# A fused convolution, four-bit FFN and expert layer on one core: an earlier start on TensorE, a reordered hand-over to the first down products, and a shorter routing step

## What is computed

```python
# layer 0
h = conv1d(x, weight, 9 taps, 4 groups) + (cond @ c_weight.T)[:, :, None] + bias
w_up, w_down = NF4[codes] * absmax                     # hidden size 2752
y = relu(h @ w_up + b_up + h @ A_up @ B_up)
x = x + y @ w_down + b_down + y @ A_dn @ B_dn
# layer 1
att = softmax(MLP(cond))                               # 8 kernels mixed per batch
z = einsum('boi,bih->boh', sum_k att_k W_k, x) + att @ bias_k
sel = argmax(z @ gate_w.T + gate_b)                    # one expert of 8 for each row
x = x + z @ expert_w[sel].T + expert_b[sel]
```

## Time and profile before

| | |
|---|---|
| timed runs | 1392.38, 1395.85, 1396.06 us (median 1395.85) |
| profiled execution, its own time | 1392.98 us |
| its span, first to last instruction | 1391.4 us |
| PE busy | 1369.3 us (98%) |
| DVE busy | 1114.1 us (80%) |
| ACT busy | 774.9 us (56%) |
| mean granted TensorE clock | 0.997 |

### The profile page before, as it was taken

How to read it: one execution, slowest core, us unless ns; L and a number is a source line. 1 busy time by engine, 2 the same in 40 slices (tenths; PEclk the granted TensorE clock), 3 DMA queues, 4 the chain that set the end, 5 groups by cost and what they waited for, 6 DMA issues and landing times.

```text
span 1391.4 us, 20662 instructions
## 1 busy us (share of the span) xinstructions
PE 1369.3 (98%) x6810; PEld 1126.3 (81%) x6810; DVE 1114.1 (80%) x1127; ACT 774.9 (56%) x872; POOL 227.5 (16%) x251
## 2 busy tenths in 40 slices
PE   8999999999999999999999999999999899999998
PEld 7888888888888888888888888888766588888887
DVE  6869887878887788787877887878643699999996
ACT  5655545454554546445464554555216577777774
POOL 0110000000000000000000000000013257565462
PEclk9999999999999999999999999999999999999999
DMA  6854657487875788666886759876578865969962
GB/s 220 344 227 166 230 208 276 163 293 251 283 255 205 246 267 273 245 254 214 290 245 245 259 196 298 256 279 225 195 295 294 280 180 149 361 194 331 348 173 45
DMA packets 105108, 339.50 MB, mean 244 GB/s; under 512 B 15716, under 2 KB 23404, under 8 KB 105036
## 3 DMA queue, kind: packets, MB, share of 16 engines
q1 hardware_dynamic: 79122, 257.93, 49.9%
q0 software_dynamic: 25376, 80.24, 21.3%
q10 hardware_dynamic: 546, 0.50, 0.1%
HBM read 303.49 MB, written 46.14 MB: 251 GB/s over the span
## 4 chain that ended last, share of the span: by engine, by line
PE 93%; DVE 4%; issue 1%; ACT 1%; DMA 0%; ACTq 0%; POOL 0%; DVEq 0%; POOLq 0%
PE pair L1268 27%; PE pair L1269 27%; PE pair L1270 27%; PE pair L1327 3%; DVE wf L869 1%; PE pair L1603 1%; PE pair L1505 1%; PE pair L1495 1%; PE pair L1437 1%; PE pair L1340 1%; PE pair L1357 1%; PE pair L1517 1%; PE pair L1583 1%; PE pair L1320 0%; PE pair L1394 0%
## 5 line engine op out<-in xcount | busy, mean ns | idle before, releaser
L869 DVE TENSOR_TENSOR wf<-wf,term 128x1024 f32<-128x1024 f32 x308 | 376.6, 1223 | 64.3 <-ACT term L616 49.9
L616 ACT ACTIVATE term<-codes 128x1024 f32<-128x1024 int32 x308 | 320.5, 1055 | 137.2 <-DVE wf L869 137.2
L1268 PE MATMUL pair<-wh,hh 128*128 128x512 f32 x672 | 263.4, 392 | 2.1 <-DVE ring L944 1.4
L1269 PE MATMUL pair<-wl,hh 128*128 128x512 f32 x672 | 262.0, 390 | 0.0
L1270 PE MATMUL pair<-wh,hl 128*128 128x512 f32 x672 | 261.9, 390 | 0.0
L1268 PE MATMUL pair<-ring,wh 128*128 128x512 f32 x624 | 242.9, 389 | 0.0
L1269 PE MATMUL pair<-ring,wh 128*128 128x512 f32 x624 | 242.9, 389 | 0.0
L1270 PE MATMUL pair<-ring,wl 128*128 128x512 f32 x624 | 242.7, 389 | 0.0
L939 DVE TENSOR_TENSOR acc<-acc,pair 128x1024 f32<-128x1024 f32 x160 | 194.6, 1216 | 46.2 <-PE pair L1270 40.3
L803 ACT ACTIVATE whr<-wraw 128x1024 fp32r x176 | 181.7, 1057 | 63.7 <-PE pair L1270 52.1
L1242 DVE TENSOR_TENSOR wlr<-wraw,whr 128x1024 fp32r<-128x1024 f32 x176 | 203.6, 1218 | 0.9 <-issue 0.5
(11 more groups left out here) (202 smaller groups left out, 1558.9 us busy)
## 6 DMA issues: line engine op xcount, KB each, us to landing
ring<-x_parts SPq DMA_DIRECT2D x320, 512.0 KB, 6.7
wraw<-exp_w SPq DMA_DIRECT2D x64, 512.0 KB, 10.0
x_parts<-stage POOLq DMA_DIRECT2D x24, 512.0 KB, 6.7
xg<-exp_b POOLq DMA_DIRECT2D x23, 512.0 KB, 8.1
codes<-codes_up SPq DMA_DIRECT2D x22, 512.0 KB, 7.2
codes<-codes_dn SPq DMA_DIRECT2D x22, 512.0 KB, 6.8
am<-am_dn SPq DMA_DIRECT2D x22, 512.0 KB, 3.8
acc<-x_nat POOLq DMA_DIRECT2D x16, 512.0 KB, 5.3
```

Source lines behind the costliest of these rows:

```text
L616: return nc.scalar.activation(out, codes[:, n % 2], ACT.Relu, scale=scale, bias=-scale * bend)
L869: nc.vector.tensor_tensor(whole(n), whole(n), term[:, e % 2], op).then_inc(term_added, 1)
L1268: mm(ps, ah, bh, start=first, stop=False)
L1269: mm(ps, ah, bl, start=False, stop=False)
```

## The change

- The first thing on PE is nine filler matmuls. Then `conv(0)` starts with its first group, and the context product follows behind that group.
- `low(0, 1)` on DVE comes one convolution batch sooner, and ramp 1 of tile 2 one later.
- Splits of batches 24 and 25 are moved ahead of and between `high`/`low(0, 3)` and `relu`/`hidden_low(0, 1)`.
- `down(0, 0)` waits for the split of batches up to 29 before j = 0 and for all before j = 1, where it waited for all at once. In the first turn `add_down(0, 0, 0)` stands ahead of the ramps, and `add_down(0, 0, 1)` behind two.
- The gates of tiles 13, 14 and 15 write banks 0, 1 and 4; those of 13 and 14 no longer wait for bank 6.
- `ranked` is split into `places` and `digits`, `count_seen` and the marks are moved, and eight tiles instead of seven are marked after `choose(2)`. The filler matmuls between are three instead of six; the last twenty stay.
- SP holds blocks 4 to 7 of expert 1 until the second gather of rows has landed.

```diff
--- before.py
+++ after.py
@@ -303,7 +303,7 @@
         def gate_bank(t):
-            return bank[4 if t == TILES - 1 else 6]
+            return bank[{TILES - 3: 0, TILES - 2: 1, TILES - 1: 4}.get(t, 6)]
...
@@ -438,6 +438,8 @@
                         sp.wait_ge(z_ready, 2 * TILES if e else 4 * kt + 2)
+                        if e and kt == KT // 2:
+                            sp.wait_ge(zg_in[1], 16)
                     sp.dma_start(wraw[:, e % 2, kt], exp_w[e, :, kt]).then_inc(wraw_in[e % 2][kt], 16)
...
@@ -712,9 +714,11 @@
             ramps(0, 3, range(1, 8))
+            conv_high(LATE)
             high(0, 3)
+            conv_high(LATE + 1)
             relu(0, 1)
-            for k in range(LATE, B):
+            for k in range(LATE + 2, B):
                 conv_high(k)
...
@@ -971,9 +975,9 @@
                 elif k == 18:
+                    low(0, 1)
+                elif k == 19:
                     add_ramps(0, 2, (1,))
-                elif k == 19:
-                    low(0, 1)
                 else:
...
@@ -992,20 +996,21 @@
             add_lora(0, 3)
+            conv_low(LATE)
             low(0, 3)
+            conv_low(LATE + 1)
             hidden_low(0, 1)
-            for k in range(LATE, B):
+            for k in range(LATE + 2, B):
                 conv_low(k)
...
                     if isinstance(i, int) and i == k == 0:
+                        add_down(i, k, 0)
                         add_ramps(i, k + 4, (1,))
...
                         add_ramps(i, k + 4, (2,))
-                        add_down(i, k, 0)
-                        add_ramps(i, k + 4, (3, 4))
                         add_down(i, k, 1)
-                        add_ramps(i, k + 4, (5, 6, 7))
+                        add_ramps(i, k + 4, range(3, 8))
                     else:
...
@@ -1107,7 +1112,7 @@
-            def ranked(b):
+            def places(b):
...
@@ -1115,6 +1120,9 @@
                 link(nc.vector.reduce_sum(slotf[:, a:z], place[:, a:z], AX.X))
+            def digits(b):
+                a, z = BATCHES[b:b + 2]
                 link(nc.vector.tensor_copy(sloti[:, 0, a:z], slotf[:, a:z]))
...
@@ -1132,6 +1140,8 @@
                     picked(t - 2)
+                if t == TILES - 1:
+                    marked(6, 7)
                 if t > 0:
...
@@ -1156,26 +1166,29 @@
                 elif t == 8:
-                    ranked(0)
+                    places(0)
+                    digits(0)
+                elif t == 9:
                     count_seen(0)
-                elif t in (9, 10, 11):
+                    marked(0, 2)
+                elif t in (10, 11):
                     marked(2 * t - 18, 2 * t - 16)
...
                     choose(1)
+                    count_seen(1)
                 elif t == 13:
-                    ranked(1)
-                    count_seen(1)
+                    places(1)
                 elif t == 14:
-                    marked(6, 8)
-                elif t == 15:
-                    marked(8, 9)
+                    digits(1)
             logit(TILES - 1)
             picked(TILES - 2)
+            marked(7, 8)
             picked(TILES - 1)
             choose(2)
-            marked(9, 11)
-            ranked(2)
-            marked(11, TILES)
+            marked(8, 10)
+            places(2)
+            digits(2)
+            marked(10, TILES)
...
@@ -1269,12 +1282,22 @@
-            pe.wait_ge(ident_ready, 2)
             pe.wait_ge(ones_ready, 1)
-            pe.wait_ge(ctx_const, 48)
-            mm(bank[3][:, 0:CH], ct[:], cwt[:], start=True, stop=False)
-            mm(bank[3][:, 0:CH], ones[0:1, :], cbias[:], start=False, stop=True).then_inc(ctx_mm, 1)
+            def spin(ps, count, blocks=CT):
+                for _ in range(count):
+                    mm(ps[:, 0:blocks * P].rearrange("p (c n) -> p c n", n=P), ones[:].bitcast(F32R),
+                       ones[:].bitcast(F32R).rearrange("p (o n) -> p o n", o=1).broadcast_to([P, blocks, P]),
+                       start=True, stop=True)
+            def context():
+                pe.wait_ge(ctx_const, 48)
+                mm(bank[3][:, 0:CH], ct[:], cwt[:], start=True, stop=False)
+                mm(bank[3][:, 0:CH], ones[0:1, :], cbias[:], start=False, stop=True).then_inc(ctx_mm, 1)
+            spin(bank[0], 9)
...
@@ -1326,6 +1349,8 @@
                                  start=k == g == d == 0, stop=k > 0 and g == GROUPS - 1 and d == 1)
+                    if k == g == 0:
+                        context()
                 if k == 0:
...
@@ -1411,6 +1436,8 @@
                     wait(pe, acc_added, i * 32 + 4 * q + j - 1)
+                    if isinstance(i, int) and i == q == 0 and j < 2:
+                        pe.wait_ge(x1l_ready, B - 2 + 2 * j)
                     c = slice(j * P, (j + 1) * P)
...
@@ -1473,8 +1500,6 @@
                             conv(b)
-                        pe.wait_ge(x1l_ready, B)
                     else:
...
@@ -1509,7 +1534,7 @@
                 wait(pe, zt_ready, t + 1 - HALVED)
-                if t < TILES - 1:
+                if t < TILES - 3:
                     wait(pe, lt_ready, t)
...
@@ -1577,22 +1602,12 @@
-            def spin(ps, count, blocks=CT):
-                for _ in range(count):
-                    mm(ps[:, 0:blocks * P].rearrange("p (c n) -> p c n", n=P), ones[:].bitcast(F32R),
-                       ones[:].bitcast(F32R).rearrange("p (o n) -> p o n", o=1).broadcast_to([P, blocks, P]),
-                       start=True, stop=True)
-            pe.wait_ge(row_ready, 2 * 9)
-            placed(0, 9)
-            spin(bank[5], 2)
+            placed(0, 8)
+            spin(bank[5], 1)
             ranks(2)
             totals(1)
-            spin(bank[5], 4)
-            pe.wait_ge(row_ready, 2 * BATCHES[2] + 1)
-            placed(9, TILES)
+            spin(bank[5], 2)
+            placed(8, TILES)
             spin(bank[5], 20)
...
```

## The result

The changed kernel took 1386.17 us (median of four, 1384.71 to 1388.36), the kernel before 1395.13 (median of four, 1392.38 to 1396.06). The ratio on record is 0.9944 with a 95% interval of 0.9930 to 0.9959: faster by 0.56%, or 7.8 us. (The two medians by themselves are 8.96 us apart, a ratio of 0.9936.) Forecast were 1386.5 us and a range of 1382.0 to 1391.5. The span of the profiled execution fell from 1391.4 to 1383.1 us, by 8.3, where the sum of the steps was 7.8.

The account below looks back on a forecast made before the run. PE, busy 98% of the span, was taken as the bound, so only its idle and slow time could go. Terms 2.4 + 0.9 + 2.5 + 2.0 = 7.8 us, from 1394.3, gave 1386.5 us; range 1382.0 to 1391.5.

Parts of the forecast that it names:

- The start: Before batch 1: fillers raise PE's clock and context follows the first matmuls; batch 1 at about 9.4 instead of 12.0, gain 2.4 us.
- Rival A: Clock does not rise at the start and does not help at the table; gains 4.8 us, about 1389.5; chance 0.12.
- `low(0, 1)`: Hand-over to the first up product: DVE subtracts one step sooner, PE's 1.0 us wait goes; gain 0.9 us.
- Batches 28 to 31 and the first down products: Earlier splits and adds remove PE waits of 2.85 us; DVE lateness returns about 0.4; gain taken as 2.5 us.
- Routing: End of routing: table and gather 2.0 us sooner; first transposes gain 1.6 (slow fillers) to 3.1 (gather decides), taken 2.0.
- The held loads: Expert 1 loads: no gain; half held, so a gather 2 us sooner does not meet their tail.
- Rival B: DVE becomes the bound behind the first down products; gain falls to 5.6 us, about 1388.7; chance 0.10.
- Rival C: Fewer fillers before the table leave the clock at 1.2 GHz when expert tiles begin; slower, 1400; chance 0.03.
- Rival D: Whole kernel: waits only move and nothing is won, within 0.3%, 1392 to 1396; chance 0.05.

## Why the prediction was right, step by step

The time was right to 0.3 us, and part of that is luck. The forecast took the kernel before at 1394.3, and it measured 1395.13; the gain was 7.8 us forecast and 7.8 by the ratio, 8.3 in the profiles and 9.0 by the medians. The terms were less exact, and two errors cancelled: 0.8 us too much for the down products, 1.0 too little for routing. Of the marks forecast, batch 1 (9.4) came at 9.71, the table (1098) at 1098.54, the first transposes (1104.6) at 1104.45; the one new wait for `acc` came where said, but with 1.30 us and not 0.4.

- **The start**, 2.4 forecast, 2.27 measured. The mechanism, fillers that take the slow matmuls on themselves, is borne out by the profiles, though each kernel without fillers has only one. The prediction let two matmuls of batch 0 go out before the context product and fourteen after it; in the records it is four and twelve (0.71 and 1.60 us), since one program matmul stands as two. What was not foreseen is how far the start varies. In eleven profiles with nine fillers batch 1 started at 9.3 to 9.7 us in seven, and at 11.9 to 12.1 in four. Rival A's first half is therefore no rival but what happens in some executions. The first up product then starts at 54.6 to 55.0 (where `low(0, 1)` is early), which is even slower than 54.0, the 55.05 of before less its wait. So in those four the fillers cost 0.6 to 1.0 us where they give 2.4 to 2.8 in the seven, and that the profile of the result is one of the seven is luck. Of the kernel before only one profile is kept, so how its own start varies is not known.
- **`low(0, 1)`**, 0.9 forecast, 1.12 measured. Undoing it costs 1.17 us there and 1.12 at the end of the FFN. From the first to the second up product PE lost 0.09 us: the cover in front of `hidden_low(0, 0)` was just enough, as said.
- **Batches 28 to 31 and the first down products**, 2.5 forecast, 6.62 - 3.30 - 1.62 = 1.70 measured. Ahead were 0.85 + 1.5 + 0.5 = 2.85 forecast and 0.89 + 1.66 + 0.77 = 3.32 measured. The step that failed is "At 128.01 DVE had 1.08 us of idle time, which takes up part": the give-back was 1.62 us and not 0.4. The idle time took up only 0.36 and left 0.72. It was a wait for ACT, and ACT's `relu` stands in its own order behind a ramp that goes only as fast as DVE adds, so it moved along with DVE's lateness. In ACT's rows above only 0.25 us of the delay had been a wait for PE. DVE's lead was 4.15 us at the start of its unbroken run and 4.32 at `hidden_low` (128.01 to 123.69). A smaller part of the error is that PE's lead was 3.32 and not 2.85. The run with the adds around `hidden_low`, whose DVE work is the same, won 1.68 us back: it was the order that cost them, and no shortage of DVE time.
- **Routing**, 2.0 forecast, 2.99 measured. The table came 2.23 us sooner, against 2.0. The other 0.76 came from PE, which had been held 1.1 us by fillers before and now starts with the gather. Of my two ends, 1.6 and 3.1, I took one near the wrong one: the granted clock was 0.50 again, but it rose 3.9 us behind the first of the twenty fillers where before it had risen 5.8 behind it, so that they took 6.66 us where 7.29 had been taken. How soon it rises varied from 3.0 to 5.7 us between profiles of kernels with the change, so up to 0.7 of this term is what that profile happened to have.
- **The held loads**, no term of their own in the forecast; taking them off costs 1.0 us in one profile. The prediction had said that a gather 2 us sooner would meet the tail of the loads without the hold, and this is what came. It was the later expectation that had the hold at nothing, since it let the data of the gather begin when the loads end and did not allow for their last transfers. Part of the routing term is the hold's: without it the transposes stand 6.92 us behind the table, 0.25 worse than before (6.67).
- **Rival B** was right in kind: DVE's lateness was the largest single error, 1.62 us given back for 0.4. It did not go all the way: DVE's own lead over the kernel before was 4.15 us at the start of its unbroken run (104.00 to 99.85), and PE kept 5.00 at the first mixing product.
- **Rival C** did not happen: the granted clock was 0.50, 1.2 GHz, from about 1095 to 1102 and 1.00 for the first expert tile. Its premise did: with fewer fillers the clock fell some 3.6 us ahead of the table, before the change 1.8. Rival D did not happen.

## What to carry to other kernels

An idle time of an engine is a reserve only if what ends it does not depend on that engine. Follow the releaser back: here the wait for ACT hung on ramps that waited for DVE, so moving PE ahead by 3 us used 0.36 of 1.08 us. Put what empties a buffer ahead of what merely prepares a later step. And when single terms are of 1 to 3 us in 1390, compare distances between marks in profiles, and check them in several, since a stage left alone can differ by more; six timed runs could not tell 1.7 us.

## What the runs showed of the hardware that was not expected

- The clock at the start, read from the pace of the matmuls, rises either before the first convolution or only between 13 and 14 us, with the same nine fillers from 1.45 us. Seven profiles had the first, four the second, none lay between. The gap behind the fillers does not decide it: it was 0.57 to 0.99 us in the seven and 0.56 to 0.73 in the four; the difference is 2.3 us at batch 1 and some 3 at the first up product.
- The first gather of 128 rows takes 4.2 to 4.4 us from issue to landing, 5.4 behind the tail of the expert loads (one profile), and gathers between 1170 and 1200 us, on full queues, take 9 to 13 us.
- Behind small matmuls the clock rose 3.0 to 5.8 us after the first of a run of fillers, in all fourteen profiles before the fillers ended.
- The length of the expert stage, from its first product to the end, varied from 275.6 to 282.9 us between profiles of kernels whose code for it is the same but for the hold. The longest is one without the hold, but the kernel before, also without it, took 276.9. This is a spread nearly as large as the whole gain of the change. In the two longest steps, of 15.2 and 15.9 us, the granted clock fell to 0.50 behind a wait of 2.0 and 2.2 us.
